# Gathers without the small writes behind them, and GpSimd at most two pairs of groups ahead of TensorE's sums

## What is computed

```python
def rgcn_layer(x, W, SW, b, src, dst, rel):          # stages 1 and 2, 8 relations
    xt = einsum('nd,rde->rne', x, W)
    agg = segment_sum(xt[rel, src], dst)
    return relu(agg + x @ SW + b)

x = layernorm(x + rgcn_layer(rgcn_layer(x, ...), ...))

deg = segment_sum(ones, dst)                          # stage 3
feat = relu(x @ W1 + b1)
h = feat * deg ** -0.5
agg = segment_sum(h[src], dst)
x = layernorm(x + (feat - agg * deg ** -0.5) @ W2 + b2)
```

## Time and profile before

| | us |
|---|---|
| three runs | 7341.99, 7342.03, 7355.17 |
| median | 7342.03 |
| span of the profiled execution | 7320.2 |
| GpSimd busy | 5851.5 |
| TensorE busy | 3691.2 |
| VectorE busy | 1720.1 |

### The profile page before, as it was taken

The page is one execution under the profiler, slowest core; times in us unless marked ns, Lnnn a source line. Parts: engine busy times, 40 slices in busy tenths (PEclk is TensorE's granted clock), DMA queues, the critical chain, the costliest instruction groups (busy, mean ns, idle before and its releaser), DMA issues.

```text
span 7320.2 us, 56431 instructions
## 1 busy us (share of the span) xinstructions
PE 3691.2 (50%) x13687; PEld 2669.6 (36%) x13841; DVE 1720.1 (23%) x2844; ACT 409.6 (6%) x915; POOL 5851.5 (80%) x9940
## 2 busy tenths in 40 slices
PE   4555555555555556556565555554424333433343
PEld 3333333333333333334343333433323333333333
DVE  4333333333333212222222222221101111111111
ACT  1000000000000100000000000010000000000000
POOL 7888888888888588888888888867888888888887
PEclk7666667676666777767677776675555555555555
DMA  2111111111111112211222221211111111111111
GB/s 66 49 51 52 50 50 50 51 52 50 50 52 51 40 49 57 56 56 55 56 58 56 56 57 56 56 54 42 51 51 52 51 51 51 51 51 53 51 51 48
DMA packets 197585, 382.88 MB, mean 52 GB/s; under 512 B 84322, under 2 KB 93326, under 8 KB 197542
## 3 DMA queue, kind: packets, MB, share of 16 engines
q0 software_dynamic: 159456, 326.88, 17.0%
q1 hardware_dynamic: 36416, 54.67, 2.1%
q10 hardware_dynamic: 1670, 0.85, 0.0%
HBM read 356.43 MB, written 25.65 MB: 52 GB/s over the span
## 4 chain that ended last, share of the span: by engine, by line
POOL 48%; issue 20%; another core or an unknown queue 20%; PE 7%; DVE 3%; DVEq 1%; POOLq 0%; ACT 0%; DMA 0%; ACTq 0%; SPq 0%
POOL rows L794 39%; POOL pause L798 9%; PE bank L980 3%; PE bank L950 3%; DVE r_S L1042 1%; DVE r_hot L1037 1%; PE bank L1205 1%; ACT r_agg L904 0%; PE bank L1440 0%; PE bank L964 0%; DVE acc L1081 0%; DMA acc<-in_dst_dram 0%; DVEq L1071 0%; POOLq L109 0%
## 5 line engine op out<-in xcount | busy, mean ns | idle before, releaser
L794 POOL DMA_INDIRECT rows<-in_x_dram,idx x1661 | 1588.6, 956 | 466.9 <-issue 396.7
L794 POOL DMA_INDIRECT rows<-x_d,idx x1647 | 1574.2, 956 | 453.5 <-issue 397.8
L794 POOL DMA_INDIRECT rows<-h_d,idx x1640 | 1566.9, 955 | 441.4 <-issue 396.3
L980 PE MATMUL bank<-r_S,rows 128*128 128x128 f32 x6644 | 1408.2, 380 | 705.1 <-issue 486.8
L1205 PE MATMUL bank<-r_S,rows 128*128 128x64 f32 x3322 | 821.9, 388 | 1332.3 <-issue 1079.4
L980 PEld LDWEIGHTS bank<-r_S,rows 128*128 128x128 f32 x6644 | 1299.5, 285 | 501.4 <-issue 482.1
L1205 PEld LDWEIGHTS bank<-r_S,rows 128*128 128x128 f32 x3322 | 775.1, 315 | 1378.0 <-issue 1272.4
L798 POOL MEMSET pause<- 128x128 f32 x4948 | 1096.3, 222 | 4.3 <-issue 0.2
L1042 DVE TENSOR_TENSOR r_S<-bank,key 128x1792 f32<-128x1792 f32 x238 | 480.4, 2019 | 1225.9 <-remote 1080.3
L964 PEld LDWEIGHTS bank<-zeros_bf 128*128 128x128 bf16 x476 | 54.1, 114 | 1463.0 <-issue 1056.8
L964 PE MATMUL bank<-zeros_bf 128*128 128x512 bf16 x323 | 174.9, 542 | 722.4 <-issue 505.8
(11 more groups left out here) (152 smaller groups left out, 1471.1 us busy)
## 6 DMA issues: line engine op xcount, KB each, us to landing
rows<-in_x_dram,idx POOLq DMA_INDIRECT x1661, 3.3
rows<-x_d,idx POOLq DMA_INDIRECT x1647, 3.4
rows<-h_d,idx POOLq DMA_INDIRECT x1640, 3.4
d_xr<-in_x_dram SPq DMA_DIRECT2D x54, 218.0 KB
x_d<-d_yr SPq DMA_DIRECT2D x27, 218.0 KB
d_x1r<-x_d SPq DMA_DIRECT2D x27, 218.0 KB
h_d<-d_hr SPq DMA_DIRECT2D x27, 218.0 KB
part_d<-d_pr SPq DMA_DIRECT2D x27, 218.0 KB
```

The lines of the kernel that those rows point to most:

```text
L794: pool.indirect_dma_start(out=self.c.rows[:, self.place(s), :], out_offset=None, in_=self.table[:, :], in_offset=bass.IndirectOffsetOnAxis ...
L980: mm = pe.matmul(agg_ps[j][:, bass.ds(offs[j * KG + k], TK)], c.rows[:, g.place(h * KG + k), :], S[:, pb, j * KG + k, :], start=False, sto ...
```

## The change

The buffer `pause`, its memsets and the semaphore `paused` with all its waits are taken out. A constant `LEAD = 2` is new. In the first pass of a stage the wait for `summed` is as before; in all later ones it asks for the sum of the pair two before, in place of the pair four before. So the fifth pair of a stage needs the sum of the third. In the first pass, for all pairs but the first, there is a wait more, `breathe`: the pair before must have landed.

```diff
+LEAD = 2
...
-        c.pause = sb("pause", [P, PT, P])
...
-        self.rest = PAIR if then is None else 1
...
-        self.paused = sem("paused")
...
+    def breathe(self, pool, i, p):
+
+
+        pool.wait_ge(self.landed[p * PAIR - 1], (i + 1) * (KG * 16))
+        gate(pool, self.c.passed)
+
     def run(self, pool, ready, stored):
...
-        def iteration(q, i, part, set_of, skip=0):
+        def iteration(q, i, part, set_of, skip=0, first=False):
...
                 pool.wait_ge(self.idx_ready, (q * (IT + 1) + i) * PR + p + 1)
-                pool.wait_ge(self.summed, self.pairs_summed(q, i, p))
+                ahead = PR if first else LEAD
+                pool.wait_ge(self.summed, self.pairs_summed(q, i, p + PR - ahead))
                 gate(pool, self.c.passed)
+                if first and p > 0:
+                    self.breathe(pool, i, p)
                 for h in range(p * PAIR, (p + 1) * PAIR):
...
-                    if h % rest == 0:
-                        pool.wait_ge(self.paused, q * (NG // rest) + i * (RING // rest) + h // rest + 1)
-                        gate(pool, self.c.passed)
...
                         ).then_inc(self.landed[slot], 16)
-                        ins = pool.memset(self.c.pause[:, s % PT, :], 0.0)
-                    if h % rest == rest - 1:
-                        ins.then_inc(self.paused, 1)
...
-            iteration(q, 0, FULL, 0, skip)
+            iteration(q, 0, FULL, 0, skip, True)
```

More of the change, by code:

```diff
@@ L767, in early @@
             ).then_inc(then.landed[t // KG], 16)
+    def breathe(self, pool, i, p):
+        pool.wait_ge(self.landed[p * PAIR - 1], (i + 1) * (KG * 16))
+        gate(pool, self.c.passed)
     def run(self, pool, ready, stored):
-        rest = self.rest
-        def iteration(q, i, part, set_of, skip=0):
+        def iteration(q, i, part, set_of, skip=0, first=False):
             at = set_of * UN
@@ L776, in iteration @@
                 if (p + 1) * PT <= skip:
-                    pool.sem_inc(self.paused, PAIR // rest)
                     continue
                 pool.wait_ge(self.idx_ready, (q * (IT + 1) + i) * PR + p + 1)
-                pool.wait_ge(self.summed, self.pairs_summed(q, i, p))
+                ahead = PR if first else LEAD
+                pool.wait_ge(self.summed, self.pairs_summed(q, i, p + PR - ahead))
                 gate(pool, self.c.passed)
+                if first and p > 0:
+                    self.breathe(pool, i, p)
                 for h in range(p * PAIR, (p + 1) * PAIR):
-                    if (h + 1) * KG <= skip:
-                        if h % rest == rest - 1:
-                            pool.sem_inc(self.paused, 1)
-                        continue
-                    if h % rest == 0:
-                        pool.wait_ge(self.paused, q * (NG // rest) + i * (RING // rest) + h // rest + 1)
-                        gate(pool, self.c.passed)
                     for k in range(part.of(h)):
@@ L828, in run @@
         pool.end_ifs()
-        pool.wait_ge(self.paused, rounds * (NG // rest) + 1)
-        gate(pool, self.c.passed)
         if self.then is not None:
```

## The result

The changed kernel takes 7385.62 us (median; 7379.32 to 7400.53) where the kernel before takes 7344.53 beside it (7341.99 to 7355.17): 1.0057 times as long, 95% interval 1.0042 to 1.0072. The forecast was 7014, faster; the end of the range, 7540, was not reached.

The account below looks back on a forecast made before the run. The prediction took GpSimd's gathering as the bound, with the ring of four pairs second. 7320.2 - 438 - 378 - 79 + 75 - 25 gave 6475; +517 for pauses made 6992, and 22 from span to median 7014 us; range 6490 to 7540.

Parts of the forecast that it names:

- What bounds the kernel: Whole kernel: GpSimd, busy 80% of 7320.2 us, is the first limit; the ring of four pairs the second.
- the ring's pauses: GpSimd's old pauses at four pairs, 58 us in stage 3 and 20 in stage 1, fall away: -79 us.
- Parts 1 and 2: GpSimd's gathers: memsets gone, 4948 x 0.089 = -438 us; rests gone before 591 first gathers, -378 us.
- Part 4: Stage starts: the fifth pair waits for the third pair's sum, +75 us, bounds +30 and +102.
- Part 5: Stage ends: with a lead of at most two TensorE has less to finish, -25 us, bounds 0 and -50.
- Part 6: Steady passes, some 345 pairs: limit of two makes a 3.0 us pause at every second pair, +517 us.
- How TensorE runs beside it: Stage 3: TensorE's matmuls run slowly while GpSimd gathers, 16 per 20 us, and catch up when it pauses.
- D: Rival, chance 0.25: slower, the limit of two holds GpSimd 3.0 us at each of 345 pairs, 7532 us.
- A: Rival, chance 0.20: TensorE keeps up without memsets and rests, or is never two behind; 6497 us.
- E: Rival, chance 0.05: TensorE's granted clock leaves 0.50 for 1.0 and pauses halve, +258, 6755 us.

Follow-up runs that it names:

- e12: Kernel before with the limit of two pairs only in the last three pairs of each stage, on the prompt chip: 7150.44 us, 0.9999 times before.
- e7: Changed kernel with only four of fourteen tiles of each pair multiplied, the rest left out of the sums: 7263.2 us, one run.
- e16: Changed kernel with four of fourteen tiles of each pair multiplied, again, on a later late chip: 7238.88 us, one run.
- e1: Changed kernel with LEAD = 4 instead of 2, on a late chip: 7437.06 us, 1.0318 times before.
- e11: Changed kernel with its memsets put back, no rests, limit of two kept, no landing waits, on the prompt chip: 6734.19 us, 0.9416 times before.
- e15: Changed kernel with every other gather replaced by a memset of the same length, on a late chip: 5428.69 us, one run.
- e18: Kernel before with a rest ahead of each group in stage 3 too, on a late chip: 7372.88 us, 1.0022 times before.
- e14: Changed kernel with memsets put back, no rests, limit of two kept, no landing waits, on a late chip: 7530.71 us, 1.0253 times before.
- e8: Changed kernel with gathers of 128 rows of 128 bytes instead of 512: 7378.79 us, one run.
- e17: Changed kernel with rests put back by one memset per group, limit of two kept, no landing waits: 7458.26 us, 1.0137 times before.

## Why the prediction was wrong

**What bounds the kernel.** I read GpSimd's 80% and its 48% of the chain as the bound, and the ring's pauses as a small term of 79 us. But some two dozen pauses in stage 3 meant that there, on the average of many pairs, the sums already came no faster than the gathers: 2396 / 119 = 20.1 us a pair, while GpSimd's own pace was 19.4. A producer that reaches the end of its ring has shown the pace at which its consumer follows. The forecast's 19.0 us (17.5 and, at every second pair, 3.0 of pause) was never checked against that. (The prediction's "about 45 times" is too many for its trace: from the sixth pairs on there are 34 pauses, 11 in stage 1 and 23 in stage 3.)

**Parts 1 and 2** held: inside a pair gathers are 1.25 us apart with a gap of 0.30, and a pair that need not wait starts after 0.30. The mean from one gather of a group to the next fell from 1.356 to 1.261 us; 4948 times that difference is 467 us, 29 more than the 438 of the forecast (4948 x 0.089 is 440, to be exact). The gather rows' own fall from 956 to 948 ns is part of it.

**Part 4**, +75: the waits of the first passes and the fifth pairs came to 66 us more than before, beyond the usual gap. **Part 5**, -25: the two waits at stage ends fell from 43.4 and 26.8 to 5.2 and 17.7, and the end after the last gather from 21.8 to 19.1; 50 us, at the bound.

**Part 6** is the step that failed. The pattern that I named, a pause at every second pair, is in the rows: 0.3, 5.6, 0.3, 5.9 us for long stretches, with two in a row at times. But there were 204 pauses instead of 172, and 4.75 us beyond the gap instead of 3.0: 969 us instead of 517. I took the 3.25 us of one full ring for the price, which is the pause of a consumer that is just too slow, not of one that is mostly released only when GpSimd stops. With the measured terms, 7320 - 467 - 378 - 79 + 66 - 50 + 969 = 7381 of the 7383 of the span. The mechanism behind the pattern failed as well: part 6 has TensorE catch up in a pause and then fall behind in its matmuls, and neither is what the pauses wait for.

**How TensorE runs beside it**: I took the sparse rows of stage 3 for a TensorE held back in its matmuls, and said that no row tells why. For the kernel before that was right: the last of a pair starts 22.3 us after the last gather (4.5 in e12, on the prompt chip), and their idle time is 1079.4 us of "issue". I then carried it over to the limit of two, where it no longer holds:

```profile
L1196 PE MATMUL bank<-r_S,rows 128*128 128x64 f32 x3322 | 774.1, 416 | 1417.8 <-DMA rows<-h_d,idx 1018.5
```

TensorE now waits mostly for gathers to land. What is left is the late release, 13.7 us, and with 71% of the matmuls gone (e7, e16) the pauses stayed, so TensorE's work is not their main cause. That the releases follow GpSimd's stops was right.

**The rivals.** D was right in the sign, and the idle time before GpSimd's gathers, 2606 - 1484 = 1122 us beyond the gaps, is above the 900 that I had named as its mark. Its point of decision, a mean of 2.45 us a pair, was passed: 969 / 342 = 2.83. Its price (3.0 us at each pair) and its reason, a credit that cannot be carried, were not: 204 pauses of 4.75 us stand in place of 345 of 3.0, and with a limit of four (e1) they sum up to nearly the same. A, "TensorE keeps up", was not run on the prompt chip with the changed kernel itself; there e11 shows what it rests on, next to no pauses with a limit of two. An estimate from e11's time and part 1 of the prediction, 6734 - 438, is 6296 us, so A's 6497 would even be too high there. E: the granted clock is 0.50 in stage 3 as before and plays no part. As for what the Trainium skill says of a matmul's row ("Perfetto Trace Analysis", "Summary: the profiler window per engine type"), that its end is an estimate and the passing on of a semaphore lies outside it, the trace agrees in so far as the release came 17.3 us behind the last row's end at 1014.82; how much of this is the row's end and how much the passing on of the semaphore, no run separates.

## What to carry to other kernels

If a producer ever meets the end of its ring, compute from the stage's length the pace at which the consumer follows before you price a faster producer: here, on late chips, nothing beyond it was gained, and a smaller lead added nothing. Do not take that pace for the consumer's own, either: e15 and e18 show that it changed with how the producer spaced its work. When a wait is ended by no row ("remote") while the engine waited for had finished, cut that engine's work as an experiment; if the wait stays, look at what the other engines do at the time. And measure a pacing change in more than one place: the same kernel (e11, e14) took 0.942 and 1.025 times before in two groups.

## What the hardware showed that I had not expected

- On the late chips the release of TensorE's sums of stage 3 reached VectorE 13.7 us (after, median) and 15.9 us (before), up to 50.7 us, after the start of the last matmul, while GpSimd gathered in close order; half of the pauses in the changed kernel end 5.5 us or more after the last gather, 183 of 204 by 6. In the same program it took 0.6 us in all 119 pairs on the prompt chip (e11), and 2.3 us in the median and up to 18.4 on a late one (e14). What in the chip holds it back stays open. It hardly depends on the number of row matmuls (median 13.1 and 10.8 us in e7 and e16), nor on the bytes gathered (12.3 in e8), nor on how busy GpSimd is (0.6 in e15). It depends on how closely gathers follow each other: in stage 3 none of 119 sums came later than 0.6 us with 8 gathers in 15 us (e15), 3 came later than 1.5 with 14 in 20.04 us (e18), 94 with 14 in 19.40 (before), 103 with 14 in 17.5 and the limit of two (after).
- Why the groups differ, 7150 against 7218 to 7364 us for the same kernel, stays open too.
- A gather without a memset behind it has a gap of 0.30 us before the next, with one 0.17: 0.13 of the memset's 0.39 is not saved.
- The waits for landing in the first pass took 2 to 6 us each. In the kernels without them and with few or no rests (e14, e17) the fifth pairs waited 34 to 70 us, in the changed kernel 8 to 31. No run took the landing waits alone away, so that they are what helps is not shown.
